# A gated recurrence with its k*v products moved to GpSimd, its decay in PSUM, and one PSUM bank for the attended rows

## The chip, the cores and the metric

One NeuronCore of a Trainium2 chip runs the kernel. The metric is the device time of one execution in microseconds (us). DVE is VectorE, ACT is ScalarE, PE is TensorE, POOL is GpSimd, SP is SyncE. SBUF is the on-chip memory of 128 partitions, PSUM the accumulation memory of eight banks of 128 x 512 float32.

## The reference

Two layers follow each other on x (64 x 64 x 256, float32). The first is a cross attention per batch element with a normalisation over the batch. The second, which the change touches, is an RWKV block (B = 64 sequences, L = 64 tokens, E = 256 channels, H = 32 heads of S = 8):

```
xn = ln(x);  sx = shift(xn) - xn
xxx = tanh((xn + sx*maa_x) @ maa_w1) @ maa_w2          # five mixes
x5  = xn + sx*(maa_stack + xxx)                        # five mixed inputs
w = exp(-exp(time_decay + tanh(x5[1] @ decay_w1) @ decay_w2))
r, k, v = x5[3] @ Wr.T, x5[0] @ Wk.T, x5[2] @ Wv.T;  g = silu(x5[4] @ Wg.T)
step:  a = k_t v_t^T;  out_t = r_t (u*a + s);  s = a + w_t*s
att = groupnorm(out);  x = x + (att*g) @ Wo.T
xn2 = ln(x);  x = x + sigmoid(xr @ Wr2.T) * (relu(xk @ Wk2.T)**2 @ Wv2.T)
```

## The kernel before

`attention` (the first layer, to about 165 us) and `norm_params` come first; `rwkv` holds the second layer. It works on eight chunks (`CHUNKS`) of eight sequences, 512 tokens each. Channels lie on partitions in two halves, h = 0 and 1. For each chunk there are three groups of work: A makes the inputs of the recurrence, B is the recurrence, C is the output projection and the feed-forward part. Every engine has its own written-out order of instructions, held together by semaphores alone. In the steady state one loop body n does B of chunk n, A of chunk n+1 and C of chunk n-1. Bodies 1 to 6 are whole; body 0 has no C, and chunk 7 has a tail of its own.

The recurrence. `spread_v` (SP) copies each row of v by DMA into `vb[h]`, so that partition (head, i) meets each of the eight value channels e. One half of these channels, four of them, is a part: parts (h, q) are (0,0), (0,1), (1,0), (1,1) in that order. For each part DVE does three steps. `b_kv` (L1200) multiplies v by k into the state tile `st`, 128 x 2016. `b_scan` runs four scans of 128 x 512 (L1213), s = w*s + kv, in place. Its last instruction (L1218, 128 x 2048) multiplies by r back into `vb`. ACT writes the initial states into column 0 of `st` (`state_column`, L952). There is one `st`, so `b_kv` of a part waits for the product of the part before it (`prod_ready`). PE then sums over the key channel (`b_reduce`, L766) into one of two banks `att[h]` and adds the bonus row (`b_bonus` of PE, L772).

The bonus. DVE multiplies r, the bonus and k (`b_ruk`, L1181), PE sums over a head into a bank of its own (`b_head_sum`, L758), and DVE multiplies by v (`b_bonus` of DVE, L1186).

The mixes. PE transposes zn (`a_turn`, L698), ACT makes xn, DVE makes sx (L1161) and xm (L1164) in `a_shift`. PE multiplies by w1 (`a_mix`, L717), ACT applies tanh. For each of five mixes j PE makes two banks (`a_mod`, L731), DVE makes (bank + stack) * sx (`a_mod`, L1173, two instructions of 128 x 512), and POOL adds xn (`add_x`, L624, one instruction of 128 x 1024). Then PE projects (`a_proj`, L704), or, for j = 0, goes through `a_dec1` (L740) and `a_dec2` (L746) for the decay. ACT takes the two banks of `a_dec2` through two exponentials into w[p][h] in SBUF (`a_w`, L989 and L992).

Banks. Names of A use three banks in rotation in the order of `A_ORDER`, those of C two (`C_ORDER`). Before PE writes a bank, `a_bank` waits until the name that used it three places earlier has been read. PE's in-order queue in a body is: g projection, `a_turn`, `c_var`, head sum 0, `a_mix`, mix 0, `c_out`, head sum 1, mix 1, reduce (0,0), mix 2, `a_dec1`, reduce (0,1), `c_turn`, `a_dec2`, v projection, `c_key`, mix 3, `c_recept`, `c_value`, k projection, mix 4, reduce (1,0), r projection, bonus 0, reduce (1,1), bonus 1. `c_turn` waits for zn2, which comes from DVE's `c_x1`, POOL's `rstd` and ACT's `c_norm`; ACT then makes xn2, for which DVE's `c_shift` (L1238, L1242) waits.

DVE's order in a body is: kv and scan (0,0), `b_ruk`, `a_shift`, kv (0,1), `c_gn`, mix 0, bonus 0, scan (0,1), mix 1, `c_x1`, bonus 1, mix 2, kv (1,0), `c_shift`, scan (1,0), mix 3, `a_z` (L1155 and moments), kv (1,1), scan (1,1), `c_final` (L1252, L1256), mix 4. POOL's is: four small copies (`prev`, L620), the adds of mix 0, `rstd` (L612, L614) for C, the adds of mixes 1 to 3, `rstd` for the next chunk but one, the add of mix 4.

Of the kernel before, what the change touches and what calls it, by code (L numbers as in the profile page):

```python
# [17 lines left out]
P = 128  # L18
# [23 lines left out]
C_PROD, C_SELF, C_ONES, C_AVG, C_HALF, C_ID = 0, 8, 9, 10, 11, 12  # L42

# [23 lines left out]
def attention(nc, sem, t, d):  # L67
# [15 lines left out]
    ident = cst[:, C_ID, :]  # L83
# [7 lines left out]
    with ctx:  # L91
# [51 lines left out]
        def _(pool):  # L143
# [17 lines left out]
            first = t["cst"][:, C_ONES, 0:P:S]  # L161
# [238 lines left out]
def norm_params(nc, sem, t):  # L400
# [4 lines left out]
    with ctx:  # L405
# [52 lines left out]
def rwkv(nc, sem, t, d, out):  # L458
# [4 lines left out]
    ident, ones_head, pick, gn_eh = cst[:, C_ID, :], cst[:, C_ONES, :], t["pick"], t["gn_eh"]  # L463
# [10 lines left out]
    dec_tanh, dec_exp, w_ready = sem("decay_tanh"), sem("decay_exp"), sem("w_ready")  # L474
# [7 lines left out]
    att_sq, var_ln, gn_rstd, gn_scaled, ag_ready = sem("att_squared"), sem("var_ln"), sem("gn_rstd"), sem("att_scaled"), sem("att_gated")  # L482
# [9 lines left out]
    A_ORDER = ["g0", "g1", "T0", "T1", "m0", "m1", "w0a", "w0b", "w1a", "w1b", "w2a", "w2b", "dec1", "dec2a", "dec2b",  # L492
               "v0", "v1", "w3a", "w3b", "k0", "k1", "w4a", "w4b", "r0", "r1"]
    A_READ = {"T0": (xn_ready, 1, 2), "T1": (xn_ready, 2, 2), "m0": (mix_tanh, 1, 2), "m1": (mix_tanh, 2, 2),
              "dec1": (dec_tanh, 1, 1), "dec2a": (dec_exp, 1, 2), "dec2b": (dec_exp, 2, 2),
# [4 lines left out]
    NA = len(A_ORDER)  # L500
# [11 lines left out]
    with ctx:  # L512
# [19 lines left out]
        w = [[sb(f"w_{p}{h}", [P, NB, L]) for h in range(2)] for p in range(2)]  # L532
# [5 lines left out]
        st = sb("state", [P, 4, NB, L])  # L538
# [8 lines left out]
        sbank = pb("ps_headsum")  # L547
        att = [pb(f"ps_att{h}") for h in range(2)]
# [8 lines left out]

        def cb(name):
            return cbank[C_ORDER.index(name) % 2]

        def a_body(n, name):
            return n if name in ("g0", "g1") else n - 1

        def a_at(n, name):
            return (a_body(n, name) + 1) * NA - 2 + A_ORDER.index(name) + 1

# [42 lines left out]
        def _(pool):  # L609
# [16 lines left out]
            def body(n, a=True, c=True, z=True):  # L626
# [4 lines left out]
                if a:  # L631
                    add_x(n + 1, 0)
                if c:
                    rstd(n - 1, ln2_var, ln2_rstd, ve2, rs2)
                if a:
                    add_x(n + 1, 1)
                    add_x(n + 1, 2)
                    add_x(n + 1, 3)
                if z:
                    rstd(n + 2, ln1_var, ln1_rstd, ve1, rs1)  # L640
                if a:
                    add_x(n + 1, 4)

# [4 lines left out]
            add_x(0, 0)  # L648
            add_x(0, 1)
            add_x(0, 2)  # L650
            add_x(0, 3)
            add_x(0, 4)
            prev(1, sx_ready, xprev, t["prev1"], xn)
            add_x(1, 0)
            add_x(1, 1)
            add_x(1, 2)
            add_x(1, 3)
            rstd(2, ln1_var, ln1_rstd, ve1, rs1)
            add_x(1, 4)
            with pool.Fori(1, CHUNKS - 2) as n:  # L660
                body(n)
            body(CHUNKS - 2, z=False)

            prev(CHUNKS - 2, sx2_ready, xprev2, t["prev0"], xn2)
            rstd(CHUNKS - 2, ln2_var, ln2_rstd, ve2, rs2)
            rstd(CHUNKS - 1, ln2_var, ln2_rstd, ve2, rs2)
            prev(CHUNKS - 1, sx2_ready, xprev2, t["prev0"], xn2)

        @block.tensor
        def _(pe):  # L670
            def warm(count):
                keep_warm(nc, ident, cst[:, 0:2, :].rearrange("p a b -> p (a b)"), sbank, count)

            def a_bank(n, name):

                g = A_ORDER.index(name)
                same = [i for i in range(NA) if i % 3 == g % 3]
# [4 lines left out]
                wait(pe, s, (in_body if before in ("g0", "g1") else in_body + 1) * count + i)  # L682
# [60 lines left out]
            def a_dec2(n):  # L743
                pe.wait_ge(dec_tanh, n + 1)
                for c, name in enumerate(("dec2a", "dec2b")):
                    nc.tensor.matmul(a_bank(n, name)[:, :], low_w[DEC:2 * DEC, P * c:P * c + P], low_t[DEC:2 * DEC, :],  # L746
                                     start=True, stop=True).then_inc(a_done, 1)
# [6 lines left out]
            def b_head_sum(n, h):  # L754

                pe.wait_ge(ruk_ready, n * 2 + h + 1)
                wait(pe, bonus_ready, n * 2 + h)
                nc.tensor.matmul(sbank[:, :], ones_head, bon[h][:, :], start=True, stop=True).then_inc(head_sum, 1)  # L758

            def b_reduce(n, h, q):  # L760

                pe.wait_ge(prod_ready, n * 4 + 2 * h + q + 1)
                if q == 0:
                    wait(pe, gn_scaled, n * 2 + h - 1)
                for i in range(4):
                    mm = nc.tensor.matmul(att[h][32 * i:32 * i + 32, :], pick[:, q, :], vb[h][:, 2 * i + q, :],  # L766
# [3 lines left out]
            def b_bonus(n, h):  # L770
                pe.wait_ge(bonus_ready, n * 2 + h + 1)
                nc.tensor.matmul(att[h][:, :], turn_eh, bon[h][:, :], start=False, stop=True).then_inc(att_done, 1)  # L772
# [51 lines left out]
            def body(n, a=True, b=True, c=True):  # L824
# [60 lines left out]
            a_dec2(0)  # L885
# [6 lines left out]
            b_head_sum(0, 0)  # L892
            a_turn(1)
            b_head_sum(0, 1)
            b_reduce(0, 0, 0)
            a_mix(1)
            a_mod(1, 0)
            a_mod(1, 1)
# [3 lines left out]
            a_dec2(1)  # L902
            a_proj(1, 1, "v", WV)
            a_mod(1, 3)
            b_bonus(0, 0)
# [5 lines left out]
            b_bonus(0, 1)  # L911
            with pe.Fori(1, CHUNKS - 2, 2) as n:
# [18 lines left out]
            c_var(CHUNKS - 1)  # L931
            warm(12)
# [9 lines left out]
        def _(act):  # L942
# [5 lines left out]
            def state_column(n, h, q):  # L948

                part = 2 * h + q  # L950
                wait(act, prod_ready, n * 4 + part)
                nc.scalar.activation(st[:, :, :, 0], t["s0"][:, h, q:S:2, bass.ds(n * NB, NB)], ACT.Copy).then_inc(col_ready, 1)  # L952
# [510 lines left out]
```

## Time and profile before

| what | us |
|---|---|
| median of 3 runs (lowest to highest) | 811.88 (808.75 to 815.48) |
| profiled execution, its own time | 810.09 |
| its span in the trace | 808.3 |
| DVE busy in the span | 676.6 |
| PE busy in the span | 699.6 |
| POOL busy in the span | 207.1 |

The span is the time from the first to the last recorded instruction; 1.8 us of the execution lie around it. An instruction's time in the trace runs from its start to its end, so an instruction that is held up after its start looks longer than another of the same shape. "Idle before" is the time in which the engine had nothing running.

### The profile page before, as it was taken

The numbers are of one execution on the slowest core, as the hardware profiler recorded it, in microseconds if no ns is written. First come the engines' busy times: TensorE is split into PE (matmuls) and PEld (weight loads), VectorE is DVE, ScalarE is ACT, GpSimd is POOL, SyncE is SP. The second block draws the span as 40 slices with busy tenths as digits, with TensorE's granted clock in tenths as the row PEclk, the third lists the DMA queues.
The fourth block names the chain that finished last, engine by engine and source line by source line (L and its number), as shares of the span: only waits on it lengthen the run. The fifth ranks groups of instructions, "written<-read, shape, count | busy, mean of one in ns | idle before, by whom it ended". The sixth has DMA issues, their size and how long they took to land. (4 is left out here: it accounts for less than half of the span.)

```text
span 808.3 us, 9662 instructions
## 1 busy us (share of the span) xinstructions
PE 699.6 (87%) x2736; PEld 361.1 (45%) x2736; DVE 676.6 (84%) x1008; ACT 361.1 (45%) x789; POOL 207.1 (26%) x163
## 2 busy tenths in 40 slices
PE   7599999989969698998897899889798988956887
PEld 5356666655322234533352453335334443423475
DVE  3499999964298989998999999999989999996923
ACT  4478888822423262344336334433525344232342
POOL 2640000003304404341334334133413523230000
PEclk9699999999998799898899999979998999986999
DMA  2621212200650460533056053305603241450000
GB/s 86 200 63 52 65 52 65 65 10 18 128 106 24 81 130 1 104 90 67 3 102 156 0 104 82 73 0 104 157 0 83 63 88 26 79 130 1 0 27 26
DMA packets 38298, 54.76 MB, mean 68 GB/s; under 512 B 4578, under 2 KB 21106, under 8 KB 38146
## 3 DMA queue, kind: packets, MB, share of 16 engines
q1 hardware_dynamic: 36866, 50.46, 27.6%
q0 software_dynamic: 1408, 4.02, 1.5%
q8 instruction: 10, 0.16, 0.1%
q14 instruction: 14, 0.11, 0.1%
HBM read 16.72 MB, written 4.19 MB: 26 GB/s over the span
## 5 line engine op out<-in xcount | busy, mean ns | idle before, releaser
L624 POOL TENSOR_TENSOR x<-x,xn 128x1024 f32<-128x1024 f32 x40 | 123.0, 3083 | 284.1 <-DVE x L1173 284.1
L1213 DVE TENSOR_TENSOR_SCAN state<-w,state 128x512 f32<-128x512 f32 x128 | 168.5, 1377 | 5.7 <-ACT state L952 4.8
L704 PE MATMUL ps_a<-x,wsq 128*128 128x512 f32 x256 | 132.7, 662 | 9.3 <-DVE x L1173 6.7
L704 PEld LDWEIGHTS ps_a<-x,wsq 128*128 128x128 f32 x256 | 51.3, 211 | 89.6 <-issue 71.7
L1173 DVE SCALAR_TENSOR_TENSOR x<-ps_a,vec,sx 128x512 f32<-128x512 f32 x80 | 57.3, 745 | 33.2 <-PE ps_a L731 26.1
L1200 DVE TENSOR_TENSOR state<-vb,k 128x2016 f32<-128x2016 f32 x32 | 82.0, 2562 | 3.0 <-DMA vb<-v 3.0
L1218 DVE TENSOR_TENSOR vb<-state,r 128x2048 f32<-128x2048 f32 x32 | 73.4, 2292 | 1.7
L731 PE MATMUL ps_a<-mix_t,w 32*128 32x512 f32 x128 | 64.7, 627 | 3.7 <-DVE x L1173 3.7
L612 POOL TENSOR_TENSOR rs<-ve,mhalf 128x4 f32<-128x4 f32 x16 | 26.8, 1672 | 146.2 <-DVE ve L1149 146.2
L290 ACT ACTIVATE probs<-ps_f,negmax 128x256 f32<-128x256 f32 x128 | 59.0, 473 | 2.0 <-DVE negmax L339 1.2
L717 PE MATMUL ps_a<-zn,w 128*128 128x512 f32 (+1 forms) x64 | 39.5, 759 | 14.9 <-DVE zn L1164 14.9
L339 DVE TENSOR_REDUCE negmax<-ps_f 128x2 f32<-128x512 f32 x64 | 41.2, 685 | 5.9 <-PE ps_f L212 3.4
L349 DVE TENSOR_SCALAR probs<-probs,rowinv 128x256 f32<-128x256 f32 x128 | 43.0, 378 | 2.2
L959 ACT ACTIVATE zn<-wyz,rs 128x256 f32<-128x256 f32 (+1 forms) x64 | 33.2, 589 | 24.3 <-POOL rs L614 23.8
L212 PE MATMUL ps_f<-thph 32*128 32x256 f32 x256 | 37.2, 406 | 6.9 <-ACT probs L290 6.8
L731 PEld LDWEIGHTS ps_a<-mix_t,w 32*128 32x128 f32 x128 | 20.7, 185 | 45.4 <-issue 35.3
L758 PE MATMUL ps_headsum<-bonus,cst 128*128 128x512 f32 x32 | 19.1, 680 | 23.6 <-DVE bonus L1181 21.1
L235 PE MATMUL ps_av<-probsT,gz 128*64 128x256 f32 x256 | 35.5, 397 | 3.8 <-issue 2.5
L766 PE MATMUL ps_att<-vb,pick 128*32 128x512 f32 x256 | 35.9, 638 | 1.5 <-DVE vb L1218 1.5
L222 PE MATMUL ps_t<-cst,probs 128*128 128x128 f32 x256 | 36.3, 285 | 0.7 <-DVE probs L349 0.7
L800 PE MATMUL ps_c<-wsq,ag 128*128 128x256 f32 x128 | 34.6, 395 | 0.0
L212 PEld LDWEIGHTS ps_f<-thph 32*128 32x128 f32 x256 | 24.4, 188 | 21.1 <-issue 19.5
(161 smaller groups left out, 1194.9 us busy)
## 6 DMA issues: line engine op xcount, KB each, us to landing
vb<-v SPq DMA_DIRECT2D x128, 256.0 KB, 5.8
x<-in_x SPq DMA_DIRECT2D x32, 128.0 KB, 2.1
c<-in_ctx SPq DMA_DIRECT2D x32, 128.0 KB, 2.1
x_chunk<-in_x SPq DMA_DIRECT2D x8, 512.0 KB, 7.6
out<-sx SPq DMA_DIRECT2D x8, 512.0 KB, 2.9
wsq<-in_wsq POOLq DMA_DIRECT2D x1, 1024.0 KB, 8.4
cst<-in_cst POOLq DMA_DIRECT2D x1, 768.0 KB, 4.4
wsq<-in_wsq POOLq DMA_DIRECT2D x1, 768.0 KB, 8.7
```

The source lines that it names most:

```text
L212: mm = nc.tensor.matmul(ps_f[e][:, T * i:T * i + T], tp[r:r + CI, T + P * i:T + P * i + P], tp[r:r + CI, 0:T], start=True, stop=True)
L290: mm = nc.scalar.activation(pr[b][:, i, :], ps_f[e][:, T * i:T * i + T], ACT.Exp, bias=nm[b][:, i:i + 1], accum_out=rs[b][:, i:i + 1])
L339: nc.vector.tensor_reduce(nm[2 * p + e][:, :], ps_f[e][:, :].rearrange("p (i j) -> p i j", i=2), AX.X, ALU.max, negate=True).then_inc(s_ma ...
L349: nc.vector.tensor_scalar(pr[b][:, i, :], pr[b][:, i, :], ri[b][:, i:i + 1], None, ALU.mult).then_inc(s_scl, 1)
L624: nc.gpsimd.tensor_tensor(x5[j % 2][:, :, :], x5[j % 2][:, :, :], xn[:, :, 1:L1], ALU.add).then_inc(x5_ready, 1)
L704: mm = nc.tensor.matmul(bank[:, :], wsq[:, weight, c, P * o:P * o + P], src(c), start=(c == 0), stop=(c == EC - 1))
L717: mm = nc.tensor.matmul(bank[0:hi - lo, :], t["w1"][:, c, lo:hi], xm[:, TOK * c:TOK * c + TOK], start=(c == 0), stop=(c == EC - 1))
L731: nc.tensor.matmul(bank[:, :], lhs, rhs, start=True, stop=True).then_inc(a_done, 1)
L1173: nc.vector.scalar_tensor_tensor(x5[j % 2][:, NB * c:NB * c + NB, :], bt(ab(name)[:, :]), col(STK0 + MIX_OF[j], c), sx[:, NB * c:NB * c + ...
L1200: nc.vector.tensor_tensor(st[:, :, :, 1:L], src[:, :, :, 0:L - 1], wide(k[p][h][:, :])[:, :, :, 0:L - 1], ALU.mult).then_inc(kv_ready, 1)
L1213: nc.vector.tensor_tensor_scan(row, w[p][h][:, :, :].rearrange("p b t -> p (b t)"), row, 0.0, ALU.mult, ALU.add).then_inc(scanned, 1)
L1218: nc.vector.tensor_tensor(src, st[:, :, :, :], wide(r[p][h][:, :]), ALU.mult).then_inc(prod_ready, 1)
```

## The change

All of it is in `rwkv` but the loading of fewer constants (`cst` shrinks from 13 to 4 blocks, and the load of the other nine is left out).

- `b_kv` goes from DVE to POOL. There are two state tiles, `st[0]` and `st[1]`, one for each q, so that the product for a part may start when the part before the last has been multiplied by r.
- `add_x` goes from POOL to DVE, at the end of DVE's `a_mod`.
- The decay stays in PSUM: `a_dec2` writes one bank of its own for each h, ACT's exponentials run in place there, and the scans read w from PSUM. There is one w for each h (there were two in SBUF). `a_dec2` for h = 1 moves to the end of PE's body, `a_w` for h = 1 to ACT's next body.
- The two banks for this come from the attended rows, which have one bank instead of two (ACT copies it to `attc` in SBUF, and squares from there), and from the head sums, which now lie in the rotating banks of A as h0 and h1. `b_head_sum` (n, 0) goes behind `a_mix`. By the rotation w2a now follows h1, so PE writes it only after DVE's bonus 1.
- DVE's order: `a_shift` before `b_ruk`, bonus 0 before mix 0.

```diff
     A_ORDER = [... "m1", "w0a", "w0b", "w1a", "w1b", "w2a", "w2b", "dec1", "dec2a", "dec2b",
+    A_ORDER = [... "m1", "h0", "w0a", "w0b", "h1", "w1a", "w1b", "w2a", "w2b", "dec1",
-        st = sb("state", [P, 4, NB, L])
+        st = [sb(f"state_{q}", [P, 4, NB, L]) for q in range(2)]
+        attc = sb("attc", [P, 2, TOK])
-        sbank = pb("ps_headsum")
-        att = [pb(f"ps_att{h}") for h in range(2)]
+        w = [pb(f"ps_w{h}") for h in range(2)]
+        att = pb("ps_att")
...
@@ gpsimd
-            def add_x(n, j):
-                pool.wait_ge(mod_ready, n * 10 + 2 * j + 2)
-                nc.gpsimd.tensor_tensor(x5[j % 2][:, :, :], x5[j % 2][:, :, :], xn[:, :, 1:L1], ALU.add).then_inc(x5_ready, 1)
+            def b_kv(n, p, h, q):
+                if q == 0:
+                    pool.wait_ge(v_spread[h], n * 16 * S + 16 * S)
+                    pool.wait_ge(k_ready, n * 2 + h + 1)
+                src = vb[h][:, q:S:2, :].rearrange("p e (b t) -> p e b t", t=L)
+                wait(pool, prod_ready, n * 4 + 2 * h + q - 1)
+                nc.gpsimd.tensor_tensor(st[q][:, :, :, 1:L], src[:, :, :, 0:L - 1], wide(k[p][h][:, :])[:, :, :, 0:L - 1],
+                                        ALU.mult).then_inc(kv_ready, 1)
+            def body(n, p, a=True, b=True, c=True, z=True):
+                if a:
+                    prev(n + 1, sx_ready, xprev, t["prev1"], xn)
+                if c:
+                    prev(n - 1, sx2_ready, xprev2, t["prev0"], xn2)
+                if b:
+                    b_kv(n, p, 0, 1)
+                    b_kv(n, p, 1, 0)
+                if c:
+                    rstd(n - 1, ln2_var, ln2_rstd, ve2, rs2)
+                if b:
+                    b_kv(n, p, 1, 1)
+                if z:
+                    rstd(n + 2, ln1_var, ln1_rstd, ve1, rs1)
+                if a:
+                    b_kv(n + 1, q, 0, 0)
@@ tensor
+            def a_dec2(n, h):
+                pe.wait_ge(dec_tanh, n + 1)
+                wait(pe, scanned, (n - 1) * 16 + 8 * h + 8)
+                nc.tensor.matmul(bt(w[h][:, :])[:, :, 1:L], ...)
             def body(n, a=True, b=True, c=True):
...
+                if a:
+                    a_mix(n + 1)
                 if b:
                     b_head_sum(n, 0)
                 if a:
-                    a_mix(n + 1)
                     a_mod(n + 1, 0)
...
                 if b:
                     b_reduce(n, 0, 1)
+                    b_bonus(n, 0)
                 if c:
                     c_turn(n - 1)
                 if a:
-                    a_dec2(n + 1)
+                    a_dec2(n + 1, 0)
...
                 if b:
-                    b_bonus(n, 0)
                     b_reduce(n, 1, 1)
                     b_bonus(n, 1)
+                if a:
+                    a_dec2(n + 1, 1)
@@ scalar
+            def b_att(n, h):
+                act.wait_ge(att_done, n * 2 + h + 1)
+                wait(act, gn_scaled, n * 2 + h - 1)
+                nc.scalar.activation(attc[:, h, :], att[:, :], ACT.Copy).then_inc(att_copied, 1)
@@ vector
             def a_mod(n, j):
...
+                dve.wait_ge(mod_ready, n * 10 + 2 * j + 2)
+                nc.vector.tensor_tensor(x5[j % 2][:, :, :], x5[j % 2][:, :, :], xn[:, :, 1:L1], ALU.add).then_inc(x5_ready, 1)
             def b_scan(n, p, h, q):
...
-                    nc.vector.tensor_tensor_scan(row, w[p][h][:, :, :].rearrange("p b t -> p (b t)"), row, 0.0,
+                    nc.vector.tensor_tensor_scan(row, w[h][:, :], row, 0.0,
                                                  ALU.mult, ALU.add).then_inc(scanned, 1)
...
             def body(n, p, a=True, b=True, c=True, z=True):
                 if b:
-                    b_kv(n, p, 0, 0)
                     b_scan(n, p, 0, 0)
-                    b_ruk(n, p)
                 if a:
                     a_shift(n + 1)
                 if b:
-                    b_kv(n, p, 0, 1)
+                    b_ruk(n, p)
                 if c:
                     c_gn(n - 1, q)
+                if b:
+                    b_bonus(n, 0)
                 if a:
                     a_mod(n + 1, 0)
                 if b:
-                    b_bonus(n, 0)
                     b_scan(n, p, 0, 1)
```

In the tail DVE now does scan (0,0), `b_ruk`, scan (0,1), `c_gn`, bonus 0, scan (1,0), `c_x1`, bonus 1, `c_shift`, scan (1,1), `c_final`.

## Rows read from the trace of the kernel before

**Rows 1.** The page: TensorE's granted clock in 40 slices of the span, in tenths.
```profile
PEclk9699999999998799898899999979998999986999
```

**Rows 2.** Windows: five periods between sx instructions; length, busy by engine, PEclk, DMA.
```profile
438.10:507.65 69.55, 61.70 (x193) 27.75 (x192) 68.45 (x81) 29.79 (x52) 24.61 (x13) 0.98 0.35 75
507.65:580.65 73.00, 66.15 (x193) 30.01 (x192) 68.08 (x80) 29.90 (x52) 24.59 (x13) 0.91 0.34 72
...
sum 360.34, PE 325.39 PEld 146.50 DVE 341.74 ACT 150.65 POOL 123.01; mean PE 65.08 PEld 29.30 DVE 68.35 ACT 30.13 POOL 24.60
```

**Rows 3.** Groups by line and form: busy us, mean ns of one | idle before.
```profile
L624 POOL TENSOR_TENSOR x<-x,xn 128x1024 f32<-128x1024 f32 x40 | 123.0, 3083 | 284.1 <-DVE x L1173 284.1
L1200 DVE TENSOR_TENSOR state<-vb,k 128x2016 f32<-128x2016 f32 x32 | 82.0, 2562 | 3.0 <-DMA vb<-v 3.0
...
L1161 DVE TENSOR_TENSOR sx<-xn 128x1024 f32<-128x1024 f32 x8 | 9.8, 1220 | 5.7 <-ACT xn L972 5.7
...
L186 POOL TENSOR_TENSOR s<-s,sum_s 128x1024 f32<-128x1024 f32 x1 | 2.4, 2354 | 0.0
```

**Rows 4.** Single lines: count, ns of one as min/median/max, first and last start.
```profile
L1213 DVE TENSOR_TENSOR_SCAN state<-w,state x128: 1190/1198/3130, 223.6 to 762.0; 128x512 f32<-128x512 f32 x128
...
L1200 DVE TENSOR_TENSOR state<-vb,k x32: 2243/2249/3777, 221.2 to 755.9; 128x2016 f32<-128x2016 f32 x32
...
L624 POOL TENSOR_TENSOR x<-x,xn x40: 2160/3146/4202, 196.9 to 709.2; 128x1024 f32<-128x1024 f32 x40
...
L1173 DVE SCALAR_TENSOR_TENSOR x<-ps_a,vec,sx x80: 739/744/751, 195.2 to 708.3; 128x512 f32<-128x512 f32 x80
```

**Rows 5.** Timeline of POOL: start, us, instruction, idle before.
```profile
196.92 2.17 POOL L624 TENSOR_TENSOR x<-x,xn 128x1024 f32<-128x1024 f32 x1 [1.96 <-DVE x L1173]
...
495.53 4.12 POOL L624 TENSOR_TENSOR x<-x,xn 128x1024 f32<-128x1024 f32 x1 [9.48 <-DVE x L1173]
```

**Rows 6.** Timeline of DVE: start, us of the group, instruction, idle before.
```profile
198.20 1.61 DVE L1173 SCALAR_TENSOR_TENSOR x<-ps_a,vec,sx 128x512 f32<-128x512 f32 x2 [1.36 <-PE ps_a L731]
...
484.84 4.57 DVE L1213 TENSOR_TENSOR_SCAN state<-w,state 128x512 f32<-128x512 f32 x4
...
495.37 2.25 DVE L1200 TENSOR_TENSOR state<-vb,k 128x2016 f32<-128x2016 f32 x1
497.71 6.37 DVE L1213 TENSOR_TENSOR_SCAN state<-w,state 128x512 f32<-128x512 f32 x4
...
508.90 1.41 DVE L1164 SCALAR_TENSOR_TENSOR zn<-sx,vec,xn 128x512 f32<-128x512 f32 x2
...
516.92 1.61 DVE L1173 SCALAR_TENSOR_TENSOR x<-ps_a,vec,sx 128x512 f32<-128x512 f32 x2 [1.80 <-PE ps_a L731]
...
519.05 6.16 DVE L1213 TENSOR_TENSOR_SCAN state<-w,state 128x512 f32<-128x512 f32 x4
...
530.78 0.68 DVE L1186 TENSOR_TENSOR bonus<-ps_headsum,v 128x512 f32<-128x512 f32 x1
...
537.27 2.30 DVE L1238 TENSOR_TENSOR sx<-xn 128x1024 f32<-128x1024 f32 x1 [0.80 <-ACT xn L1030]
...
562.37 2.29 DVE L1218 TENSOR_TENSOR vb<-state,r 128x2048 f32<-128x2048 f32 x1
```

**Rows 7.** Timeline of PE, the same chunk.
```profile
510.37 5.47 PE L717 MATMUL ps_a<-zn,w 128*128 128x512 f32 x8 [2.12 <-DVE zn L1164]
...
529.30 1.93 PE L740 MATMUL ps_a<-x,dw 128*64 128x512 f32 x4
531.16 1.06 PE L766 MATMUL ps_att<-vb,pick 128*32 128x512 f32 x8
534.50 1.93 PE L698 MATMUL ps_c<-cst,zn 128*128 128x128 f32 x8 [2.27 <-ACT zn L959]
```

**Rows 8.** Timeline of ACT: the copy of k for the next chunk.
```profile
561.11 0.58 ACT L1000 ACTIVATE k<-ps_a 128x512 f32<-128x512 f32 x1
```

**Rows 9.** Waits: who waited for whom, total us, times, longest.
```profile
DVE st L1143 <- ACT wyz L1024: 13.1, 2, 7.0
```

More of the change, by code:

```diff
@@ L647, in _ @@
             rstd(1, ln1_var, ln1_rstd, ve1, rs1)
[L648 to L667, printed above, removed]
+            b_kv(0, 0, 0, 0)
+            body(0, 0, c=False)
+            with pool.Fori(1, CHUNKS - 4, 2) as n:
+                body(n, 1)
+                body(n + 1, 0)
+            body(CHUNKS - 3, 1)
+            body(CHUNKS - 2, 0, z=False)
+            body(CHUNKS - 1, 1, a=False, z=False)
+            body(CHUNKS, 0, a=False, b=False, z=False)
         @block.tensor
@@ L671, in warm @@
             def warm(count):
-                keep_warm(nc, ident, cst[:, 0:2, :].rearrange("p a b -> p (a b)"), sbank, count)
+                keep_warm(nc, ident, cst[:, 0:2, :].rearrange("p a b -> p (a b)"), att, count)
             def a_bank(n, name):
                 g = A_ORDER.index(name)
-                same = [i for i in range(NA) if i % 3 == g % 3]
+                first = isinstance(n, int) and n == 0 and name not in OWN
+                same = [i for i in range(NA) if i % 3 == g % 3 and not (first and A_ORDER[i] in OWN)]
                 at = same.index(g)
@@ L681, in a_bank @@
                 in_body = a_body(n, name) if at else a_body(n, name) - 1
-                wait(pe, s, (in_body if before in ("g0", "g1") else in_body + 1) * count + i)
+                wait(pe, s, (in_body if before in OWN else in_body + 1) * count + i)
                 return abank[g % 3]
@@ L756, in b_head_sum @@
                 pe.wait_ge(ruk_ready, n * 2 + h + 1)
-                wait(pe, bonus_ready, n * 2 + h)
-                nc.tensor.matmul(sbank[:, :], ones_head, bon[h][:, :], start=True, stop=True).then_inc(head_sum, 1)
+                if isinstance(n, int) and n == CHUNKS - 1:
+                    pe.wait_ge(gate_ready, n * 2 + 2)
+                    wait(pe, bonus_ready, n * 2 + h)
+                    bank = ab(f"h{h}")
+                else:
+                    bank = a_bank(n, f"h{h}")
+                nc.tensor.matmul(bank[:, :], ones_head, bon[h][:, :], start=True, stop=True).then_inc(head_sum, 1)
             def b_reduce(n, h, q):
@@ L884, in _ @@
             warm(2)
-            a_dec2(0)
+            a_dec2(0, 0)
+            a_dec2(0, 1)
             a_proj(0, 1, "v", WV)
@@ L911, in _ @@
             b_bonus(0, 1)
+            a_dec2(1, 1)
             with pe.Fori(1, CHUNKS - 2, 2) as n:
@@ L1099, in _ @@
             a_w(0, 0)
+            a_w(0, 1)
             a_copy(0, "v", v, v_ready)
@@ L1312, in _ @@
             a_z(1)
-            a_mod(0, 0)
-            a_mod(0, 1)
-            a_mod(0, 2)
-            a_mod(0, 3)
-            a_mod(0, 4)
-            b_kv(0, 0, 0, 0)
-            b_scan(0, 0, 0, 0)
-            b_ruk(0, 0)
-            b_bonus(0, 0)
-            b_kv(0, 0, 0, 1)
-            a_shift(1)
-            b_scan(0, 0, 0, 1)
-            a_mod(1, 0)
-            a_mod(1, 1)
-            b_kv(0, 0, 1, 0)
-            a_mod(1, 2)
-            b_scan(0, 0, 1, 0)
-            b_bonus(0, 1)
-            b_kv(0, 0, 1, 1)
-            a_mod(1, 3)
-            a_z(2)
-            b_scan(0, 0, 1, 1)
-            a_mod(1, 4)
+            for j in range(5):
+                a_mod(0, j)
+            body(0, 0, c=False)
             with dve.Fori(1, CHUNKS - 4, 2) as n:
```

164 lines of the change are left out of this document (78 added, 86 removed).

## The prediction, made before the changed kernel ran

> **What bounds the kernel now.** I read the granted clock first [rows 1], then the windows of the steady state, then the groups by line, then both timelines of one chunk. In the windows the reader is to see the period: five chunks from one sx instruction to the next take 360.3 us, 72.1 each, and DVE is busy for 68.35 of it, PE for 65.1 [rows 2]. DVE sets the pace, with PE close behind: where the clock was 0.98 the period was 69.55 us, at 0.91 it was 73.00 [rows 2].
>
> DVE's 68.35 us are not all its own work. Four scans take 4.57 us when nothing is beside them, but 6.37 and 6.16 elsewhere; a k*v has a median of 2249 ns and a longest of 3777; the sx of `c_shift` takes 2.30 against 1.22 for the same shape [rows 3 to 6]. The timelines say why. At 495.37 DVE starts a k*v; POOL starts an add at 495.53, which takes 4.12 us where 2.16 is the shortest, and ends at 499.65, two us after DVE's k*v has ended at 497.62. DVE's scans, started at 497.71, take 1.80 too long: until POOL is done. So each of the two holds the other up for the rest of the running instruction when both read two operands from SBUF. DVE's mix instructions, with one operand in PSUM, are never stretched (739 to 751 ns over 80 of them [rows 4]), also at 198.20 beside the POOL add of 196.92 to 199.09 [rows 5, 6]. The Trainium skill states this as a rule (SBUF — State Buffer, section "Who interferes with whom"): DVE with two SBUF inputs and GpSimd reading SBUF exclude each other for a whole instruction, DVE with one does not. By that rule the change frees the scans and nothing else; the trace agrees. Per period these stretches sum to 1.80 + 1.59 + 1.53 + 1.08 = 6.0 us [rows 4, 6], so that DVE's own work is 62.3 us, and 72.1 - 68.35 = 3.7 us are waits.
>
> **The change, part by part, for a whole body.**
>
> DVE's own work. Four k*v leave, 4 x 2.25 = 9.0 us. Five adds come, 128 x 1024 with both operands in SBUF, at the 1.22 of the sx instruction [rows 3] = 6.1. Scans that read PSUM are not in this trace. The bonus instruction reads PSUM and takes 0.68 for 512 columns, half of 1.22 is 0.61, so 0.07 more for each of 16, 1.1 us in all, is the upper bound. Nothing is the lower one, since the mix instructions from PSUM (744) show no premium. I take 0.6. Own work after: 62.3 - 9.0 + 6.1 + 0.6 = 60.0 us.
>
> POOL's k*v. It is not in the trace. By columns from the shortest add, 2160 x 2016/1024 = 4.25 us; from the setup's instruction with a broadcast operand, 2354 [rows 3], 4.63. The 3146 of the median add [rows 4] would give 6.2, but that holds time in which POOL was held up. I take 4.3, with 4.25 and 6.2 as ends. The Trainium skill (GPSIMD Engine Reference, section "Performance versus the Vector engine") gives 4497 ns for 2048 columns, an estimate of 4.43 here; the sum would then be some 4 us higher.
>
> Four of these make 17.2 us per body. All could vanish beside the scans, 4 x 4.57 = 18.3 us, which now contend with nothing. So the question is where each falls:
> - k*v (1,0) may start when the product of (0,0) is done. What follows on DVE is `a_shift`, `b_ruk` and the gated half of `c_gn`, all with two SBUF operands. Nothing covers it: 4.3 us.
> - k*v (1,1) may start after product (0,1), but it is queued behind POOL's `rstd`, which waits for `c_x1`. It starts some 1.3 us after that. Until then and beside it run bonus 1 (0.7), a new wait for w2a (below, 1.2) and the two mix instructions (1.4); the add is then held up by 4.3 + 1.3 - 3.3 = 2.3 us.
> - k*v (0,0) of the next chunk needs k_ready, whose first copy ended at 561.7 [rows 8], while product (1,1) started at 562.37 [rows 6]. PE sets this one, the scans of (1,1) are nearly over by then, and it stands against the product and `c_final`. Only the half of `c_final` that reads PSUM (two at 0.68) covers it: 3.0 us.
> - k*v (0,1) needs product (1,1), is queued behind that, and falls on mix 4, whose two PSUM instructions cover 1.4: 2.9 us.
> The sum is 12.5 us in the place of 6.0: the better cover of the scans is used by hardly any of them.
>
> PE's queue. Head sum 0 now goes behind `a_mix`. From the end of xm on, PE needs 5.5 us for `a_mix` [rows 7] and 1 for the head sum, while DVE has `b_ruk` 1.4 and `c_gn` 2.8: a wait of 2.3 before bonus 0, and about 1.0 more for the banks of mix 0, against 1.8 before [rows 6]. w2a must wait for DVE's bonus 1 (the rotation), so that after bonus 1 PE still has four matmuls of mix 2 (1.9), `a_dec1` (1.93), reduce (0,1) (1.06), bonus 0 (about 1), and only then `c_turn` (1.0 to 1.9) [rows 7]. That puts the end of `c_turn` about 7.5 us behind the start of bonus 1 (530.78), where it was 536.43 - 530.78 = 5.6, and PE has idled before it, so the clock may fall as it did at 534.50, where eight transposes took 1.93 us. `c_shift` then waits about 2.0 us against 0.8 [rows 6]. Queued behind PE's waiting w2a are `a_dec1`, reduce (0,1) and `c_turn`, and for these wait ACT's tanh of the decay and xn2. With 1.2 for w2a and 0.6 left for mix 3 the waits sum to 3.3 + 1.2 + 2.0 + 0.6 = 7.1 us, against 3.7.
>
> What costs nothing. ACT is busy for under half of the period (mean 30.13 of 72.1 [rows 2]), so `b_att` (two copies of 0.6) lies in its idle time; if that cover went it would be 1.2. The halves of `a_dec2` only change places in PE's queue, and the later one is needed a body later. DVE's semaphores for one att bank and one w are met early. SP's queue has the same transfers in the same order; the last spread of v is behind the store and thus behind `c_final`, but product (0,0) comes later still. If the fewer constants matter at all, it is in the first layer, whose loads end long before they are read.
>
> The sum. A whole body: 60.0 + 12.5 + 7.1 = 79.6 us against 72.1, +7.5; six of them, +45. Body 0 has no C, so its waits are shorter, but three of its four k*v still stand against two-operand work: +6. Tail: 9.0 of k*v leave DVE and no adds come, 4.3 come back as k*v (1,0) against `b_ruk`, and scan (1,0) now fills the wait for x1, 7.0 at the longest [rows 9], with something of the k*v's latency left at the end: -3. In the prologue five adds are 1 us faster each but the first k*v is 2 slower: 0. Together +48 on the profiled 810.1, 858; the median of the runs lies 1.8 higher than that execution, so 860.
>
> **The rivals.**
>
> The scans cover the products, which ends on the other side. If k comes 4 us earlier (its first copy by 557.8, when scan (1,1) starts, and not at 561.7; from about 2 us earlier on it begins to pay), k*v (0,0) falls into scan (1,1), k*v (0,1) into scan (0,0), and k*v (1,0) into a wait of `a_shift` for xn. Then a body is 60.0 + 7.1 = 67.1 us or up to 3 less if the waits stay as before: -5 to -8, times 7, with the tail -3: about 770. For it: 17.2 of 18.3 us would fit, and POOL is free. Against: the times of rows 8 and 6, and `rstd` in front of k*v (1,1).
>
> Partial cover. Two of the four hidden: -5 to -7 per body, which leaves it near zero: 812, within 1%.
>
> PE's waits alone decide, on the slower side too: with the clock down after each new idle stretch, as in the period of 73.00 against 69.55, every wait is some 2 us longer and the cover of the scans is there: 79.6 - 7 + 2, that is +2.5 per body, 828. It is slower from the point where added waits (3.4 and the clock's 2 to 3) exceed what DVE saves (2.3) and what the stretches give back.
>
> POOL is slower than I take it, at 6.2 us with strided reads: 1.9 more at each of four places, +15 per body, 910.
>
> The change does not do what it says: scans that read PSUM are held up all the same. Few products fall on them in my placing, so it would cost at most 1 to 2 per body, inside my range.
>
> **How the numbers follow.** The forecast (830 to 890) 0.52, PE's waits (815 to 835) 0.10, a slow POOL 0.06, partial cover 0.10, full cover 0.22. The range holds the forecast's own 830 to 890 and reaches down to 785: left out are most of the full cover and the slow POOL. Of the partial cover 0.04 is faster by over 1% and 0.06 within it. A measurement of this kernel tells about 1% from no change. Faster 0.26, same 0.06, slower 0.68.
>
> **What would show it.** Right: k*v on POOL about 4.3 us at the shortest and longer in the median; adds, sx or r products on DVE stretched by one to four us; scans never stretched, about 1.2 each; a wait of DVE before bonus 0 and before mix 2; a period near 80 us. Wrong: k*v of POOL that start together with the scans, in particular (0,0) beside scan (1,1); adds at 1.22 throughout; a period under 72; POOL waiting long for products.

## The result, and the profile after

The changed kernel takes 910.4 us (median of four, 906.2 to 914.8) against 811.8, a ratio of 1.121 (95% interval 1.114 to 1.129). The forecast was 860 with a range up to 890: the direction was right, and the loss of 98.6 us is twice the 48 forecast. The profiled execution has a span of 904.1 us, 95.8 more than before.

The page: busy times, and TensorE's granted clock in 40 slices, to be held against [rows 1].

```profile
PE 721.9 (80%) x2736; PEld 363.7 (40%) x2736; DVE 698.5 (77%) x1014; ACT 366.6 (41%) x805; POOL 211.7 (23%) x155
...
PEclk9999999989668979897979897979797978896899
```

The same stretch as in [rows 2], five periods between sx instructions of `a_shift` (now L1198), in the windows view: length, busy by engine, clock, DMA.

```profile
307.46:393.34 85.88, 67.23 (x194) 29.92 (x192) 71.17 (x80) 30.39 (x54) 22.98 (x12) 0.88 0.29 62
...
sum 432.24, PE 338.14 PEld 149.77 DVE 355.82 ACT 151.82 POOL 115.53; mean PE 67.63 PEld 29.95 DVE 71.16 ACT 30.36 POOL 23.11
```

A period is 86.4 us, where it was 72.1. DVE is busy for 71.16 of it (68.35 before) and waits for 15.3 (3.7 before). So 11.6 of the 14.4 us that a period has grown are idle time of the engine that set the pace. From the first scan of chunk 0 to that of chunk 1 it is 77.6 us (61.1 before), the six whole bodies take 510.4 (428.4), the tail and the prologue are 1 and 2 us shorter.

Single lines: ns of one as min/median/max. The first is POOL's product, then the scans, the adds and the products with r on DVE.

```profile
L636 POOL TENSOR_TENSOR state<-vb,k x32: 4447/4468/6077, 217.2 to 841.6; 128x2016 f32<-128x2016 f32 x32
```

```profile
L1237 DVE TENSOR_TENSOR_SCAN state<-ps_w,state x128: 1191/1198/1224, 221.8 to 853.3; 128x512 f32<-128x512 f32 x128
```

```profile
L1213 DVE TENSOR_TENSOR x<-x,xn x40: 1224/1225/4584, 189.5 to 805.6; 128x1024 f32<-128x1024 f32 x40
```

```profile
L1242 DVE TENSOR_TENSOR vb<-state,r x32: 2291/2292/6399, 226.4 to 854.5; 128x2048 f32<-128x2048 f32 x32
```

The product takes 4.45 us. Scans that read PSUM have no premium and are never stretched, where their longest was 3130 ns [rows 4]; instead the product with r, which was never stretched before, now is, by up to 4.1 us.

DVE's timeline of one body (start, us of the group, idle before it), then POOL's.

```profile
311.98 5.64 DVE L1248 SCALAR_TENSOR_TENSOR ag<-attc,gn_eh,sq 128x512 f32<-128x512 f32 x2 [0.52 <-ACT sq L1041]
...
333.43 0.68 DVE L1225 TENSOR_TENSOR bonus<-ps_a,v 128x512 f32<-128x512 f32 x1
341.74 1.41 DVE L1210 SCALAR_TENSOR_TENSOR x<-ps_a,vec,sx 128x512 f32<-128x512 f32 x2 [7.63 <-PE ps_a L743]
...
346.97 1.23 DVE L1262 TENSOR_TENSOR sx<-xn 128x1024 f32<-128x1024 f32 x1 [2.56 <-ACT xn L1052]
...
363.62 4.57 DVE L1237 TENSOR_TENSOR_SCAN state<-ps_w,state 128x512 f32<-128x512 f32 x4
368.22 6.32 DVE L1242 TENSOR_TENSOR vb<-state,r 128x2048 f32<-128x2048 f32 x1
...
375.66 4.87 DVE L1280 SCALAR_TENSOR_TENSOR sx<-sx,wyz 128x512 f32<-128x512 f32 x2
...
393.34 1.23 DVE L1198 TENSOR_TENSOR sx<-xn 128x1024 f32<-128x1024 f32 x1 [3.43 <-ACT xn L987]
```

```profile
312.37 4.70 POOL L636 TENSOR_TENSOR state<-vb,k 128x2016 f32<-128x2016 f32 x1 [13.98 <-DMA vb<-v]
...
334.84 4.45 POOL L636 TENSOR_TENSOR state<-vb,k 128x2016 f32<-128x2016 f32 x1
...
367.92 4.47 POOL L636 TENSOR_TENSOR state<-vb,k 128x2016 f32<-128x2016 f32 x1 [2.87 <-ACT k L1017]
...
374.93 4.45 POOL L636 TENSOR_TENSOR state<-vb,k 128x2016 f32<-128x2016 f32 x1
```

Three of the four products stand against DVE: (1,0) against the first half of `c_gn` (5.64 where 1.41 is its own, +4.23), (0,0) against the product with r (+4.03), (0,1) against `c_final` (+3.58), 11.8 us together. The scans at 363.62 end just as k arrives. The half of `c_gn` that (1,0) holds up had an operand in PSUM in the kernel before, and the change itself took it away, since `ag` is now made from `attc` in SBUF. In the trace before, its line was:

```profile
L1224 DVE SCALAR_TENSOR_TENSOR ag<-ps_att,gn_eh,sq x16: 739/742/751, 297.6 to 773.6; 128x512 f32<-128x512 f32 x16
```

No run here puts that operand back into PSUM, so what it is worth by itself is not shown.

The fourth, (1,1) at 334.84, lies in DVE's idle time of 7.63 us. That idle time is the largest single item, and the forecast had 1.2 us for it. DVE's waits in the five periods (total us, times, longest):

```profile
DVE x L1210 <- PE ps_a L743: 37.7, 5, 7.6
DVE sx L1198 <- ACT xn L987: 22.0, 6, 5.0
DVE sx L1262 <- ACT xn L1052: 12.3, 5, 2.6
DVE ag L1248 <- ACT sq L1041: 2.6, 5, 0.5
```

L743 is `a_dec1`: mix 2 waits for it, not for its own banks. DVE's `a_mod` holds one more wait than the rotation: mix 2 writes x5[0], which mix 0 filled and `a_dec1` reads (`X5_READ_BY`). In PE's queue `a_dec1` stands behind mix 2, whose w2a now waits until bonus 1 has read the bank of h1. PE's timeline, and the window in which both run:

```profile
334.26 3.75 PE L734 MATMUL ps_a<-mix_t,w 32*128 32x512 f32 x4 [4.27 <-DVE bonus L1225]
337.94 3.68 PE L743 MATMUL ps_a<-x,dw 128*64 128x512 f32 x4
...
344.69 1.09 PE L701 MATMUL ps_c<-cst,zn 128*128 128x128 f32 x8 [0.28 <-ACT zn L974]
```

```profile
333.40:341.70 8.30, 7.44 (x12) 2.07 (x16) 0.71 (x3) 0.00 (x0) 5.62 (x3) 0.50 0.00 0
```

PE had been idle for 4.27 us. The granted clock of the window was 0.50, its lower level of 1.2 GHz, and `a_dec1` took 3.68 us where it took 1.93 at the upper one, at a granted clock of 1.00 [rows 7].

### The profile page after: what moved, and what is told of

The parts are those of the page before. It is cut to its first block, busy times and chain, and to the rows that moved or that the text cites. A ratio compares the mean times of both kernels' runs of the same rounds, so it can differ in the third digit from the quotient of the medians.

```text
span 904.1 us, 9712 instructions
## 1 busy us (share of the span) xinstructions
PE 721.9 (80%) x2736; PEld 363.7 (40%) x2736; DVE 698.5 (77%) x1014; ACT 366.6 (41%) x805; POOL 211.7 (23%) x155
## 4 chain that ended last, share of the span: by engine, by line
DVE 27%; PE 23%; issue 21%; ACT 6%; POOL 1%; DMA 1%; DVEq 1%; SPq 0%; ACTq 0%; POOLq 0%
DVE state L1237 12%; PE ps_a L707 5%; PE ps_a L734 4%; DVE x L1210 4%; PE ps_a L743 3%; PE ps_a L720 2%; DVE st L1180 2%; ACT zn L974 2%; PE ps_c L795 2%; PE ps_att L775 1%; DVE sx L1262 1%; ACT xn L1052 1%; PE ps_c L707 1%; DVE wyz L1192 1%; PE ps_c L809 1%
## 5 line engine op out<-in xcount | busy, mean ns | idle before, releaser
L636 POOL TENSOR_TENSOR state<-vb,k 128x2016 f32<-128x2016 f32 x32 | 147.0, 4594 | 217.6 <-DMA vb<-v 155.4
L1237 DVE TENSOR_TENSOR_SCAN state<-ps_w,state 128x512 f32<-128x512 f32 x128 | 145.9, 1202 | 6.4 <-POOL state L636 6.4
L734 PE MATMUL ps_a<-mix_t,w 32*128 32x512 f32 x128 | 76.8, 726 | 39.9 <-DVE bonus L1225 39.9
L1242 DVE TENSOR_TENSOR vb<-state,r 128x2048 f32<-128x2048 f32 x32 | 99.5, 3110 | 1.7
L619 POOL TENSOR_TENSOR rs<-ve,mhalf 128x4 f32<-128x4 f32 x16 | 16.1, 1009 | 309.8 <-DVE ve L1186 309.8
L1213 DVE TENSOR_TENSOR x<-x,xn 128x1024 f32<-128x1024 f32 x40 | 58.4, 1460 | 1.4
L1017 ACT ACTIVATE r<-ps_a 128x512 f32<-128x512 f32 x16 | 9.6, 597 | 100.9 <-PE ps_a L707 100.9
L775 PE MATMUL ps_att<-vb,pick 128*32 128x512 f32 x256 | 41.5, 730 | 6.5 <-DVE vb L1242 6.5
L1046 ACT ACTIVATE wyz<-ps_c 128x512 f32 (+1 forms) x16 | 9.6, 597 | 81.8 <-PE ps_c L809 81.8
L807 PE MATMUL ps_c<-wyz,cst 128*128 (+1 forms) x64 | 24.5, 470 | 19.8 <-DVE ag L1252 19.7
## 6 DMA issues: line engine op xcount, KB each, us to landing
wsq<-in_wsq POOLq DMA_DIRECT2D x1, 768.0 KB, 7.1
```

The source lines that it names most:

```text
L636: nc.gpsimd.tensor_tensor(st[q][:, :, :, 1:L], src[:, :, :, 0:L - 1], wide(k[p][h][:, :])[:, :, :, 0:L - 1], ALU.mult).then_inc(kv_ready, 1)
L734: nc.tensor.matmul(bank[:, :], lhs, rhs, start=True, stop=True).then_inc(a_done, 1)
L775: mm = nc.tensor.matmul(att[32 * i:32 * i + 32, :], pick[:, q, :], vb[h][:, 2 * i + q, :], start=(q == 0), stop=False)
L1213: nc.vector.tensor_tensor(x5[j % 2][:, :, :], x5[j % 2][:, :, :], xn[:, :, 1:L1], ALU.add).then_inc(x5_ready, 1)
L1237: nc.vector.tensor_tensor_scan(row, w[h][:, :], row, 0.0, ALU.mult, ALU.add).then_inc(scanned, 1)
L1242: nc.vector.tensor_tensor(src, st[q][:, :, :, :], wide(r[p][h][:, :]), ALU.mult).then_inc(prod_ready, 1)
```

## The experiments

Theory A is the explanation under test: two causes that add up. One is the rotation (bonus 1, w2a, `a_dec1`, mix 2). The other is where POOL's products fall, since each excludes a DVE instruction with two SBUF operands. Its rivals put the whole loss on one of the two, or on the decay in PSUM. Each run was timed in rounds beside the kernel before.

**Head sum 1 late.** It goes behind `a_dec1` in the rotation and in PE's queue, bonus 1 behind mix 2 on DVE.

```diff
-    A_ORDER = [... "m1", "h0", "w0a", "w0b", "h1", "w1a", "w1b", "w2a", "w2b", "dec1",
+    A_ORDER = [... "m1", "h0", "w0a", "w0b", "w1a", "w1b", "w2a", "w2b", "dec1", "h1",
```

> The changed kernel with head sum 1 placed behind dec1 in the rotation and in TensorE's queue, and bonus 1 behind mix 2 on VectorE, so that w2a no longer waits for bonus 1. Theory A (two causes, of which one is the rotation: w2a waits for bonus 1, dec1 stands behind w2a, and mix 2 on VectorE may not overwrite its input buffer before dec1 has read it): the idle time of 7.6 us before mix 2 falls under 1.5 us in each body; the product (1,1), which now lies in that idle time, stretches an add by some 2 to 3 us instead; net 4 to 6 us per body, seven bodies: 865 to 885 us. Rival B (the GpSimd products are the whole loss, and VectorE would wait at that place or at the next for something else): 900 us or more.

Measured: 873.1 us, ratio 1.071 (1.063 to 1.079), a period of 80.7. It lies in theory A's range and not in rival B's. The stretch of the add is larger than expected (4.29 us), for product (1,1), no longer covered, now stands against it nearly in full. DVE's timeline:

```profile
414.50 1.41 DVE L1209 SCALAR_TENSOR_TENSOR x<-ps_a,vec,sx 128x512 f32<-128x512 f32 x2
415.95 5.51 DVE L1212 TENSOR_TENSOR x<-x,xn 128x1024 f32<-128x1024 f32 x1
```

No idle time before mix 2 (it was 7.63), and an add of 5.51 us where 1.22 is its own.

**Small products.**

```diff
-                nc.gpsimd.tensor_tensor(st[q][:, :, :, 1:L], src[:, :, :, 0:L - 1], ...
+                nc.gpsimd.tensor_tensor(st[q][:, :, 0:1, 1:L], src[:, :, 0:1, 0:L - 1], ...
-                    nc.vector.tensor_tensor_scan(row, w[h][:, :], row, 0.0,
+                    nc.vector.tensor_tensor_scan(row, w[h][:, :], vb[h][:, 2 * i + q, :], 0.0,
```

> The changed kernel with the rotation left as it is, but GpSimd multiplies one sequence of eight only (252 columns instead of 2016) and the scans read v in the place of k*v: that part of the computation is left out. Theory A: the stretches of VectorE's two-operand instructions (11.9 us per body) nearly vanish, the 7.6 us before mix 2 stay, the wait of the shift for xn grows by 2 to 4: 835 to 860 us. Rival C (the rotation is the whole loss, the products lie beside waits anyway): 890 us or more. Rival B: about the time before or less, 815 or under.

Measured: 826.0 us, ratio 1.015 (1.008 to 1.022). It is 9 us under theory A's range, but far from both rivals. DVE's waits in its bodies say that the rotation is untouched:

```profile
DVE x L1210 <- PE ps_a L743: 38.0, 5, 7.6
DVE sx L1262 <- ACT xn L1052: 12.3, 5, 2.6
DVE sx L1198 <- ACT xn L987: 11.7, 5, 3.7
```

The wait for xn has halved where theory A let it grow, so about half of it too came from the products (see below, after the run with products beside the scans).

**Product back on DVE, add back on POOL**, the rest of the change left; then the same with head sum 1 late.

```diff
+                if b:
+                    b_kv(n, p, 0, 0)        # on VectorE, ahead of each b_scan
                     b_scan(n, p, 0, 0)
...
+            def add_x(n, j):                # on GpSimd, as before the change
```

> The changed kernel with k*v back on VectorE (with both state tiles) and the add of xn back on GpSimd; decay in PSUM, one att bank and head sums in the rotation stay. Theory A: scans are never stretched (1.2 us each), adds on GpSimd stretch only k*v and sx, and the 7.6 us before mix 2 stay; a period of 75 to 78 us: 830 to 850 us. Rival B (the products on GpSimd are the whole loss): 812 or less. Rival C (the rotation is all): 890 or more.

> Both: k*v back on VectorE and the add on GpSimd, and head sum 1 behind dec1. Left of the change: the decay in PSUM, one att bank, two state tiles. Theory A: VectorE's own 62.3 us plus 0 to 1, stretches 2.6 in the place of 6.0, waits near the 3.7 of before: 69 us a body, 785 to 800 us, faster than before by 1.5 to 3%. Rival D (reading the decay from PSUM, or the att bank that is shared, has a price of its own): 815 or more.

Measured: 824.3 us, ratio 1.014 (1.007 to 1.022), and 791.2 us, ratio 0.972 (0.965 to 0.979). The first is 6 us under theory A's range, the second inside it. The second is faster than the kernel before, so the PSUM decay and the shared att bank together gain, and rival D's price of them is out. A small price of one of them, outweighed by the other's gain, is not. The four kernels make a square: the rotation costs 37.3 us with the products on POOL (910.4 - 873.1) and 33.1 without (824.3 - 791.2); the move of the products (with the add going the other way) costs 86.1 and 81.9. The causes add up to within about 4 us here.

**The same products, beside the scans.** Product (0,0) goes to DVE. POOL's other three wait for the semaphore of the last DVE instruction ahead of a scan.

```diff
+                if (h, q) == (0, 1):
+                    pool.wait_ge(x5_ready, n * 5 + 5)
+                elif (h, q) == (1, 0):
+                    if not last:
+                        pool.wait_ge(x5_ready, n * 5 + 6)
+                elif not (isinstance(n, int) and n == 0):
+                    pool.wait_ge(xr_ready, n * 2)
...
```

> Head sum 1 late (as in the first run), product (0,0) on VectorE, and GpSimd's three other products each released by the last VectorE instruction ahead of a scan: (0,1) beside scan (0,0), (1,0) beside scan (0,1), (1,1) beside scan (1,0). Adds of xn stay on VectorE. Theory A (a product costs what it excludes, not its length): the same products of 4.45 us now stretch nothing or under 1 us a body, own work 62.2, waits 3 to 5; a period of 66 to 69 us, 770 to 795 us. Rival E (GpSimd's work slows VectorE wherever it lies, or a product that is released later is late for its scan): 830 or more.

Measured: 795.2 us, ratio 0.976 (0.970 to 0.982), at the upper end of theory A's range (0.2 over it) and far from rival E: 78 us under the run with head sum 1 late. Three of its four products have the same size and lie elsewhere; the fourth has gone back to DVE, and the 78 us hold both steps. The products, then DVE's three largest waits:

```profile
L645 POOL TENSOR_TENSOR state<-vb,k x24: 4451/4478/6547, 225.2 to 741.9; 128x2016 f32<-128x2016 f32 x24
```

```profile
DVE sx L1280 <- ACT xn L1057: 16.8, 6, 2.9
DVE bonus L1230 <- PE ps_a L773: 13.1, 6, 2.3
DVE sx L1203 <- ACT xn L992: 3.0, 1, 3.0
```

The wait of `a_shift` for xn is down to one of 3.0, from 19.0 with head sum 1 late alone. PE's r projection needs a bank that mix 4 reads; the g projection, the turn and xn come behind it. So from mix 4's first instruction to `a_shift` a chain on PE and ACT runs beside DVE's own work. PE's first step of that chain in the changed kernel, and then the window from mix 4 to `a_shift` (length, busy time of PE, PEld, DVE, ACT and POOL, clock, DMA) in three kernels: the changed one, the one with small products, the one with products beside scans.

```profile
381.25 3.37 PE L707 MATMUL ps_a<-x,wsq 128*128 128x512 f32 x4 [9.41 <-DVE x L1210]
```

```profile
380.45:393.34 12.89, 12.09 (x36) 4.95 (x36) 9.40 (x9) 5.66 (x9) 0.00 (x0) 0.86 0.65 151
```

```profile
437.69:449.20 11.51, 10.71 (x36) 4.45 (x36) 9.40 (x9) 5.66 (x9) 0.00 (x0) 1.00 0.72 170
```

```profile
425.58:437.35 11.77, 11.62 (x37) 4.46 (x36) 11.58 (x11) 6.51 (x10) 6.34 (x1) 0.97 0.73 171
```

Over five bodies these windows have a mean of 13.7 us with 9.4 of DVE's work in the changed kernel, 11.8 with 9.4 with small products, and 11.8 with 11.6 with products beside scans. So the wait of 4.4 us has two halves. One is the clock: the products that hold up the r product and `c_final` delay mix 4, PE is idle for 9.4 us (2.1 with small products), and the granted clock of the window is 0.76 to 0.86 in place of 1.00, which small products have in four bodies of five. In this way they cost once as a stretch and again as part of this wait. The other half is that product (0,0) no longer gives DVE 2.25 us of work behind mix 4. At full clock the chain takes 11.5 us, DVE has 9.4 to do, and the rest is idle; with the product back on DVE it has 11.6, and the wait is gone.

**Where the decay lies**, with products beside scans, and with the product back on DVE. The second exponential writes an SBUF tile, which the scans read.

```diff
-                nc.scalar.activation(wh, wh, ACT.Exp, scale=-1.0)
+                nc.scalar.activation(bt(ws[h][:, :])[:, :, 1:L], wh, ACT.Exp, scale=-1.0)
-                    nc.vector.tensor_tensor_scan(row, w[h][:, :], row, 0.0,
+                    nc.vector.tensor_tensor_scan(row, ws[h][:, :], row, 0.0,
```

> As the run with products beside scans, but the second exponential writes the decay to SBUF and the scans read it there; nothing else changes. Theory A (two operands in SBUF exclude a GpSimd instruction, one does not): each of three products holds up a scan by up to 4.5 us, 9 to 13 us a body, 840 to 870 us. Rival F (where the decay lies makes no difference to scans beside products): within 8 us of the other run.

> As the run with the product back and head sum 1 late (791.2 us), but the decay is written to SBUF and read there by the scans: what is left is two state tiles, one att bank and the late head sum. Theory A: adds on GpSimd stretch scans again, 2 to 3.5 us a body: 806 to 815 us. Rival G (the gain of that run came from the two state tiles or the order, not from PSUM): 785 to 797.

Measured: 897.2 us, ratio 1.103 (1.096 to 1.109), and 825.9 us, ratio 1.015 (1.008 to 1.021). DVE's scans in the first of the two:

```profile
379.42 8.57 DVE L1256 TENSOR_TENSOR_SCAN state<-w,state 128x512 f32<-128x512 f32 x4 [0.19 <-DVE state L1238]
...
404.73 8.79 DVE L1256 TENSOR_TENSOR_SCAN state<-w,state 128x512 f32<-128x512 f32 x4
...
433.92 8.81 DVE L1256 TENSOR_TENSOR_SCAN state<-w,state 128x512 f32<-128x512 f32 x4
...
450.90 4.57 DVE L1256 TENSOR_TENSOR_SCAN state<-w,state 128x512 f32<-128x512 f32 x4
```

Four scans with a product beside them take 8.6 to 8.8 us, the four without one 4.57. The place of one operand is worth 102 us (897.2 - 795.2) with the products on POOL and 34.7 (825.9 - 791.2) with the adds there, so rivals F and G are out. Both times lie over theory A's ranges, by 27 and 11 us. All 128 scans of the first run and of its counterpart, by count, busy time and mean ns:

```profile
L1256 DVE TENSOR_TENSOR_SCAN state<-w,state 128x512 f32<-128x512 f32 x128 | 242.0, 1950 | 5.7 <-POOL state L646 4.7 <-DVE state L1238 0.4
```

```profile
L1255 DVE TENSOR_TENSOR_SCAN state<-ps_w,state 128x512 f32<-128x512 f32 x128 | 146.0, 1203 | 5.7 <-POOL state L645 4.7 <-DVE state L1237 0.4
```

So 96 of the 102 us are longer scans (12.5 in a body); in the other pair it is 28.4 of 34.7.

One thing stays open. The run of 825.9 us is 14 us slower than the kernel before, though both read the decay from SBUF. Its period is 72.0 us, as before; in its profile the excess lies in front and behind (the first scan at 231.8 and not 223.6 us, body 0 +3.8, the tail +3.2). What is left of the change there, a single w for each h, one att bank and the order, may have a price outside the whole bodies. No run separates it.

**Both small products and the late head sum.**

> Head sum 1 late, and GpSimd multiplies one sequence of eight only while the scans read v in the place of k*v (left out: seven eighths of k*v). Theory A (rotation and products add up): 826 less 33 to 37, 787 to 795 us, 80 us under the same kernel with whole products. Rival H (the two overlap, each wait hides the other's): 805 or more.

Measured: 780.4 us, ratio 0.961 (0.956 to 0.967), 7 us under the range and against the rival. It is 93 us under the same kernel with whole products, and 45.6 under the run with small products alone (826.0 - 780.4).

**The rotation left, products beside the scans.**

> The changed kernel with its rotation untouched (w2a waits for bonus 1), but the products beside the scans as in the run of 795.2 us, and (0,0) on VectorE. Theory A (rotation and products add up): the 7.5 us before mix 2 are back, the stretches are not: 795 plus 33 to 37, 825 to 835 us. Rival I (the wait before mix 2 came from products that held up GpSimd, TensorE or the clock): 800 to 812.

Measured: 839.0 us, ratio 1.031 (1.026 to 1.035), 4 us above the range. DVE's largest wait in it:

```profile
DVE x L1216 <- PE ps_a L749: 38.0, 5, 7.6
```

Rival I is out. The rotation costs 44 us here, with no product in its way, so that the wait before mix 2 is its own. Over the four pairs of runs its price is 33 to 46 us.

**What is left on DVE.** z and its moments go ahead of the second shift, their power on POOL ahead of product (1,1); then, besides, head sum 0 goes ahead of the mix matmuls and `b_ruk` ahead of `a_shift`.

```diff
+                if z:
+                    a_z(n + 2)
                 if c:
                     c_shift(n - 1)
```

> The run with products beside scans (795.2 us), with z and its moments ahead of the second shift, into the 2.8 us that VectorE waits there for xn2, and its power on GpSimd ahead of product (1,1). Theory A (VectorE sets the pace, and its idle time is what is left to win): 2.8 us less in each of six bodies, 775 to 785 us. Rival J (TensorE, busy 65 us of the period, is the bound by now): 790 or more.

> As the run before it, and head sum 0 ahead of the mix matmuls again (in the rotation too), b_ruk ahead of the shift as before the change. Theory A: the wait of 2.2 us before bonus 0 goes, 1.4 come back as xm is that much later: 1 us a body or a little less, 768 to 785 us. Rival K (the mix chain through TensorE and ScalarE is the longest there, so that 1.4 later costs 1.4): 3 to 10 us slower than the run before it.

Measured: 777.5 us, ratio 0.955 (0.950 to 0.960), and 772.3 us, ratio 0.947 (0.940 to 0.954). Both beat both kernels, and rivals J and K are out. The four times of the second lie between 768.0 and 783.9 us, and its ratio leaves the highest out. The last step is not told apart from nothing, as the intervals meet. The windows' sum of the first over five periods, each 65.1 us:

```profile
sum 325.45, PE 304.49 PEld 138.50 DVE 308.31 ACT 153.08 POOL 107.77; mean PE 60.90 PEld 27.70 DVE 61.66 ACT 30.62 POOL 21.55
```

DVE is busy for 61.66 of 65.1 us with next to no stretch, PE for 60.90: little is left for either.

## Why the prediction was right or wrong

Right: that DVE and POOL exclude each other where both read two SBUF operands; that POOL's product takes about 4.3 us (4.45); that scans from PSUM are never held up; that the products would miss the scans. For reading PSUM the forecast took 0.6 us, and it costs nothing, its lower bound: DVE's own work was to be 60.0 us, and 71.16 - 11.8 leaves 59.4. The 12.5 us of stretches in a whole body (11.8 measured) are right in part by luck: product (1,1), priced at 2.3, cost nothing, and the other three cost 11.8 where 10.2 were forecast.

Wrong: the waits, 7.1 us in the forecast and 15.3 in the trace. Three terms.

- "With 1.2 for w2a": the wait before mix 2 is 7.6. This is the step that failed most. The forecast saw that `a_dec1` is queued behind w2a, and counted it for `c_turn`, but it did not see that DVE's mix 2 itself waits for `a_dec1`, which frees x5[0]. The chain holds four matmuls of w2 and `a_dec1` in the place of w2a alone. At the forecast's own prices for them, 1.9 and 1.93, that is 3.8 us; at a granted clock of 0.50 they took 7.4. The run with head sum 1 late took this wait away and 37 us with it. The trace of the kernel before already shows the dependence, at mix 2 of body 0, where L740 is `a_dec1`:

```profile
253.74 1.41 DVE L1173 SCALAR_TENSOR_TENSOR x<-ps_a,vec,sx 128x512 f32<-128x512 f32 x2 [2.42 <-PE ps_a L740]
```

- No wait of `a_shift` for xn was in the sum. It is 22.0 us in the five periods, 4.4 each. The runs with small products and with products beside the scans showed its two halves: products that delay mix 4, which the forecast charged as stretches only, and product (0,0) itself, whose 2.25 us the forecast took off DVE in full, though they lay beside PE's chain behind mix 4. That chain went unfollowed.
- "A wait of 2.3 before bonus 0, and about 1.0 more for the banks of mix 0" did not come (0.5 in all), as the stretched `c_gn` lay in that time. It made the error smaller by 2.8. Where nothing stretches `c_gn`, in the run with products beside the scans, the wait before bonus 0 is there (2.2).

And the cover of product (1,1) was taken as 3.3 us, with 2.3 left; the long wait covered it whole. Body 0 was put at +6, with shorter waits, and was +16.5: it has the wait of 7.5 before mix 2 as well (at 267.39 in its DVE timeline), one of 6.2 before bonus 0 (1.5 before), and four stretches of 14.4 together. The sum for a whole body was thus +7.5, and it is +14.4.

The rivals: the cover of the scans (770) did not occur by itself. The run that forced it, with head sum 1 late besides, gave 795.2, and with the z moved 777.5; with the rotation of the change it gave 839.0. What stood against it was the release of the products, not their length, and behind that the rotation. The 812 of the partial cover does not follow from its own terms, which leave +0.5 to +2.5 in a body and so some 815 to 830. A slow POOL gave 910 for a cause that is not there (4.45 us, not 6.2). PE's waits alone (828) is near the 826.0 of the run with small products and the rotation kept, but its own condition, whole products under the cover of the scans, is nearer to that of the run of 839.0.

## What to carry to other kernels

When a name is put into a rotation of banks, follow every wait behind the matmul that it delays, down to the buffers of the consumer that are free only when a later instruction in the same queue has read them: here a wait of one bank moved a whole chain into DVE's idle time. Look for that wait in the trace of the kernel before, also in its first body. The work on GpSimd that reads SBUF cost VectorE here by where it fell, not by its length; release such work by a semaphore just ahead of VectorE instructions that have an operand in PSUM, and give the operand that makes them so a place there. Where an engine's work lies beside a chain of another engine, taking it away gives back only what exceeds the chain: count the length of the chain before the saving. And where a stretch delays the start of a chain on TensorE, look at what the idle time does to the clock of that chain.

## What the runs showed of the hardware

Moving one operand of the scans from SBUF to PSUM changed the kernel by 102 us with all other work the same, since no PSUM scan was ever stretched (longest 1224 ns) and each product beside SBUF scans delayed them by 4.0 to 4.2 us, nearly its whole 4.45. A product that comes while a scan from SBUF runs is let in between two scans of the group: the one below came 0.24 us after the start of the first scan, at 404.73, waited for its end, and the second scan took 5.43 us where 1.19 is its own.

```profile
404.97 5.24 POOL L646 TENSOR_TENSOR state<-vb,k 128x2016 f32<-128x2016 f32 x1 [21.41 <-DVE x L1219]
```

In the group at 379.42 the product had waited for DVE's k*v, got in ahead of the first scan, and that one took 5.22. The scan itself is no slower from PSUM: the median is 1198 ns from either.

TensorE's idle time came back as slower matmuls behind it. After 4.27 us of it the granted clock was 0.50 over the next two steps, and `a_dec1` took 3.68 us in place of 1.93. After 9.4 us of it the chain behind mix 4 had a granted clock of 0.76 to 0.86, and took 12.9 to 14.5 us in place of the 11.5 at 1.00.
